# Expert stage of a four-layer network on one core: scatter before the hidden products, GpSimd multiplying the weights in, queries and scores two chunks ahead

## The chip, the cores and the metric

The kernel runs on one core of a Trainium2 chip. Its time is the device time of one execution in microseconds; the median of three runs counts. The names of the engines in the rows: PE is TensorE (PEld its weight loads), DVE is VectorE, ACT is ScalarE, POOL is GpSimd, SP the engine that issues the DMAs here.

## What is computed

The network is a chain of a bottleneck convolution, a spatial attention, a causal attention with the product-key expert layer below, another attention and a mixture of experts, on 16 images of 14 x 14 positions, 3136 tokens of 256 channels. The change touches only the product-key expert layer:

```python
def _L2_ffn_ref(x, norm_w, wq, keys, expert_down, expert_up):
    inv = jax.lax.rsqrt(jnp.mean(x * x, axis=-1, keepdims=True) + EPS)
    x_norm = x * inv * norm_w
    q = (x_norm @ wq).reshape(B, T, HEADS, 2, DIM_KEY)            # 8 heads, 2 x 32
    sim = jnp.einsum('bthpd,hkpd->pbthk', q, keys)                # 64 keys a half
    s1, i1 = jax.lax.top_k(sim[0], K)                             # K = 16
    s2, i2 = jax.lax.top_k(sim[1], K)
    all_idx = (i1[..., :, None] * NUM_KEYS + i2[..., None, :]).reshape(B, T, HEADS, K * K)
    all_scores = (s1[..., :, None] + s2[..., None, :]).reshape(B, T, HEADS, K * K)
    final_scores, pk = jax.lax.top_k(all_scores, K)
    final_idx = jnp.take_along_axis(all_idx, pk, axis=-1)
    hidden = jnp.einsum('btd,bthkd->bthk', x_norm, expert_down[final_idx])
    hidden = jax.nn.gelu(hidden, approximate=False)
    hidden = hidden * jax.nn.relu(final_scores)
    return jnp.einsum('bthk,bthkd->btd', hidden, expert_up[final_idx])
```

The kernel gathers nothing: it computes the hidden value of all 4096 experts for each token, and multiplies it with a matrix of weights that is zero but for the 128 chosen ones.

## The kernel before

`peer_ffn` holds the stage. 3136 tokens are 12 chunks of 256 tokens (two tiles of 128) and one of 64. Each engine has its own hand-written order of work, a function `chunk` that `chunks` calls: two chunks written out, a loop over pairs, then the last ones. Semaphores tie the engines together. Within an engine everything runs in the order in which it is written.

What one chunk n needs, and who does it:

- **Queries and scores** (`queries`, L1608, and `scores`, L1617, on TensorE; copies L1737 and L1744 on ScalarE): done for chunk n + 1 between the scatters of chunk n.
- **Search** (`top_halves`, VectorE, L1847 to L1854): for each tile the 16 best of 64 keys in 16 groups, by rounds of max, index and replace. Then GpSimd adds the candidates (`candidates`, L1552), VectorE searches them and makes the codes (`make_codes`, up to L1961) with the index steps of GpSimd (`index_steps`, L1557 to L1563).
- **Turn** (`turn`, L1639): TensorE transposes the codes of a tile, three transposes; ScalarE copies them out (L1780) into the bf16 rows `a_t`, `b_t` and `wh_t`; VectorE makes the low part `wl_t` of the weights (`low_weights`, L1966). There is one PSUM bank `tr_ps`, so the second tile's turn waits for the copies of the first and for its low weights.
- **Hidden** (`hidden`, L1630, 16 pairs of 4 matmuls; `hidden_out`, L1768): one pair after another into the four banks `x_ps`, Gelu from PSUM to `g`.
- **One-hots and scatter** (`one_hots`, L1988 to L1995, on VectorE; `scatter`, L1654 and L1655, on TensorE): 64 tokens (a `hb`) at a time, four of them in a chunk, each in four quarters, one `x_ps` bank a quarter. The weights of the experts of 16 tokens then lie in a bank.
- **Weights into g**: for the first two `hb` VectorE multiplies bank by bank (`weigh`, L2002, four behind the parts of the next one-hots). For the last two ScalarE copies the bank to `m_copy` (which is `qt`, L1790) and GpSimd multiplies it in (L1579).
- **Experts out** (`experts_out`, L1665, 64 matmuls into `out_ps`) and the addition to x (L2029) on VectorE.

TensorE's order in a chunk is: 10 pairs of hidden, the turns of both tiles, 6 pairs of hidden, scatter 0 with the queries behind it, scatters 1 and 2 with the scores behind them, scatter 3, experts out. VectorE's: low weights of tile 0, one-hots 0, low weights of tile 1, one-hots 1 to 3, both searches of the next chunk, its codes, the addition. A profile shows each matmul of hidden and experts out as two records, so each has 128 a chunk.

Of the kernel before, what the change touches and what calls it, by code (L numbers as in the profile page):

```python
# [7 lines left out]
ALU = mybir.AluOpType  # L8
# [6 lines left out]
P = 128  # L15
# [3 lines left out]
KC = C // P  # L19
# [1340 lines left out]
def peer_ffn(nc, x, xn_dram, mean_w, w, ident):  # L1360
# [15 lines left out]
    J = 32  # L1376
    HT = TT // 2
    NHB = 2 * NTILE
    LATE = NHB // 2
# [9 lines left out]
    with Scope(nc, "peer") as S:  # L1389
# [11 lines left out]
        m_copy = [qt[:, 2 * p:2 * p + 2, :].rearrange("p m t -> p (m t)") for p in range(2)]  # L1401
# [35 lines left out]
        g_done_late, m_copied = S.sem("g_done_late"), S.sem("m_copied")  # L1437
        halves_done, cand_ready = S.sem("halves_done"), S.sem("cand_ready")
# [3 lines left out]
        pad = S.sb("pad", [1, 1 + 3 * NTILE])  # L1442
# [19 lines left out]
        EARLY = 10  # L1462
# [7 lines left out]
        def chunks(eng, chunk):  # L1470

            for p in range(2):
                chunk(p, p, CT, CT)
            with eng.Fori(1, NCHUNK // 2 - 1) as i:
                for p in range(2):
                    chunk(2 * i + p, p, CT, CT)
            for p in range(2):
                chunk(NCHUNK - 2 + p, p, CT, CT if p == 0 else REST)
            chunk(NCHUNK, 0, REST, 0)
# [46 lines left out]
        def _(pool):  # L1526
# [38 lines left out]
            def next_tables(n, tiles):  # L1565

                for t in range(len(tiles)):
                    candidates(n, t)
                index_steps(n)

            next_tables(0, tile_rows(CT))

            def chunk(n, p, now, then):

                for hb in range(LATE, now // HT):
                    for q in range(4):
                        pool.wait_ge(m_copied, 4 * (NHB - LATE) * n + 4 * (hb - LATE) + q + 1)
                        ts = slice(hb * HT + q * GT, hb * HT + (q + 1) * GT)
                        nc.gpsimd.tensor_tensor(g[:, :, ts], g[:, :, ts], m_copy[q % 2].rearrange("p (t j) -> p j t", j=J),  # L1579
                                                ALU.mult).then_inc(g_done_late, 1)  # L1580
                if then > 0:
                    next_tables(n + 1, tile_rows(then))
# [3 lines left out]
        def _(pe):  # L1586
# [34 lines left out]
            def hidden(n, p, pairs, cols):  # L1621
                for jp in pairs:
                    b = jp % 4
                    if jp < 4:
                        wait(pe, m_copied, 4 * (NHB - LATE) * n - 3 + jp)
                    else:
                        pe.wait_ge(gelu_done, NPAIR * n + jp - 3)
# [14 lines left out]
            def scatter(n, hb):  # L1642

                pe.wait_ge(oh_ready, NHB * n + hb + 1)
                for q in range(4):
                    if hb == 0:
                        pe.wait_ge(gelu_done, NPAIR * (n + 1))
                    elif hb < LATE + 1:
                        pe.wait_ge(g_done, 4 * LATE * n + 4 * (hb - 1) + q + 1)
                    else:  # L1650
                        pe.wait_ge(m_copied, 4 * (NHB - LATE) * n + 4 * (hb - 1 - LATE) + q + 1)
# [6 lines left out]
            def experts_out(n, cols):  # L1658
                n_hb = cols // HT
                pe.wait_ge(g_done, 4 * LATE * n + 4 * min(LATE, n_hb))  # L1660
                pe.wait_ge(g_done_late, 4 * (NHB - LATE) * n + 4 * max(0, n_hb - LATE))
# [41 lines left out]
            def chunk(n, p, now, then):  # L1703
                hidden(n, p, range(EARLY), now)
                for t, rows in enumerate(tile_rows(now)):
                    turn(n, t, rows)
                hidden(n, p, range(EARLY, NPAIR), now)
                next_rows = tile_rows(then)
                for hb in range(now // HT):
                    scatter(n, hb)  # L1710
                    if hb == 0 and then > 0:
                        queries(n + 1, 1 - p, then)
                    if 0 < hb <= len(next_rows):
                        scores(n + 1, hb - 1, next_rows[hb - 1])
                experts_out(n, now)
# [3 lines left out]
        def _(act):  # L1719
# [21 lines left out]
            def score_out(n, t, rows):  # L1741
                act.wait_ge(sim_done, NTILE * n + t + 1)
                for b in range(2):
# [21 lines left out]
            def hidden_out(n, pairs, cols):  # L1765
                for jp in pairs:
                    act.wait_ge(h_done, NPAIR * n + jp + 1)
                    nc.scalar.activation(g[:, 2 * jp:2 * jp + 2, 0:cols], x_ps[jp % 4][:, 0:2 * CT].rearrange("p (j t) -> p j t", j=2)[:, :, 0:cols],  # L1768
                                         ACT.Gelu).then_inc(gelu_done, 1)

            def chunk(n, p, now, then):
                wait(act, out_done, n)
                hidden_out(n, range(EARLY), now)
                for t, rows in enumerate(tile_rows(now)):
                    act.wait_ge(tr_done, NTILE * n + t + 1)
                    ts = slice(t * TT, t * TT + rows)
                    if t == 0:
                        wait(act, oh_ready, NHB * n)
                    for dst, c in ((wh_t, 2), (a_t, 0), (b_t, 1)):
# [701 lines left out]
```

## Time and profile before

| | |
|---|---|
| three runs | 2382.08, 2389.36, 2386.52 us; median 2386.52 |
| span of the profiled execution | 2389.1 us |
| expert stage, about | 550 to 1862 us |
| busy: TensorE, VectorE, ScalarE, GpSimd | 79%, 70%, 28%, 19% of the span |
| granted TensorE clock, mean | 0.877 |

A row of a timeline gives the start in us, the time in us that a run of like instructions covers, engine, line, operation, output and inputs by name, shape, and in brackets how long the engine had been idle and on whom it waited. Instructions of an engine overlap by some 0.1 us, so the distance of two starts is what an instruction costs. In a row of windows the clock is the third number from the end: 1.00 is 2.4 GHz, 0.50 is 1.2 GHz.

### The profile page before, as it was taken

To read this page: it belongs to the slowest core of one execution; us is meant where nothing else is said; L and a number is where in the kernel's file an instruction comes from. 1 tells how busy PE (TensorE), PEld (TensorE's weight loads), DVE (VectorE), ACT (ScalarE), POOL (GpSimd) and SP (SyncE) were. 2 spreads that over 40 slices of the span, in tenths; PEclk is the share of its full clock that TensorE was granted. 3 is DMA by queue.
4 is the path that set the end of the run, shared out by engine and by line. 5 is a ranking of instruction groups with operands and counts; after the bars stand their busy time and mean duration, and the time that the engine had idled before them with its cause. 6 is when DMAs were issued, how large, how long until landed. Compare 5 with 4: busy or idle time off the path is not lost. (4 is left out here: it accounts for less than half of the span.)

```text
span 2389.1 us, 47903 instructions
## 1 busy us (share of the span) xinstructions
PE 1889.5 (79%) x17539; PEld 1539.2 (64%) x17539; DVE 1684.3 (70%) x6987; ACT 669.6 (28%) x1493; POOL 462.3 (19%) x667
## 2 busy tenths in 40 slices
PE   6595899996479788797787977978769699747995
PEld 3364688874468677686676866767658577544653
DVE  3433666645899999999999999999996477430112
ACT  1342355544222131121311213112120255421220
POOL 2002344330020201202112021120220311021111
PEclk8796899998789899898998988989888799858997
DMA  2232444413400000000000000000000233212434
GB/s 60 70 97 59 113 104 106 99 34 113 102 6 5 2 6 1 6 6 1 6 2 6 5 2 6 1 6 2 1 2 1 60 86 83 68 68 82 141 103 122
DMA packets 90420, 110.24 MB, mean 46 GB/s; under 512 B 27168, under 2 KB 79088, under 8 KB 89552
## 3 DMA queue, kind: packets, MB, share of 16 engines
q1 hardware_dynamic: 84672, 99.09, 15.8%
q0 software_dynamic: 3344, 6.53, 0.8%
q8 instruction: 140, 2.29, 0.4%
q10 hardware_dynamic: 2176, 1.61, 0.2%
q14 instruction: 88, 0.72, 0.1%
HBM read 69.84 MB, written 33.83 MB: 43 GB/s over the span
## 5 line engine op out<-in xcount | busy, mean ns | idle before, releaser
L1665 PE MATMUL peer_out_ps<-peer_g,peer_up 128*128 128x256 f32 (+1 forms) x1664 | 379.0, 393 | 85.1 <-issue 77.1
L1665 PEld LDWEIGHTS peer_out_ps<-peer_g,peer_up 128*128 128x128 f32 x1664 | 326.7, 203 | 133.8 <-issue 85.2
L1630 PE MATMUL peer_x_ps<-peer_xc,peer_dt 128*128 128x256 f32 (+1 forms) x1664 | 352.7, 373 | 19.6 <-DMA peer_up<-in_L_ffn_expert_up_dram 19.5
L1630 PEld LDWEIGHTS peer_x_ps<-peer_xc,peer_dt 128*128 128x128 f32 x1664 | 306.8, 191 | 60.3 <-issue 20.6
L1579 POOL TENSOR_TENSOR peer_g<-peer_g,peer_qt 128x512 f32<-128x512 f32 x96 | 153.0, 1636 | 796.0 <-ACT peer_qt L1790 796.0
L1768 ACT ACTIVATE peer_g<-peer_x_ps 128x512 f32<-128x512 f32 (+1 forms) x208 | 119.1, 573 | 637.1 <-PE peer_x_ps L1630 637.0
L1284 DVE TENSOR_REDUCE l_attn_mx<-l_attn_s_ps 98x4 f32<-98x392 f32 (+1 forms) x320 | 175.0, 560 | 142.7 <-PE l_attn_s_ps L1054 101.6
L1654 PE MATMUL peer_x_ps<-peer_oh_h,peer_oh_a 128*128 128x32 bf16 x3136 | 171.5, 181 | 111.2 <-DVE peer_oh_l L1995 95.6
L1654 PEld LDWEIGHTS peer_x_ps<-peer_oh_h,peer_oh_a 128*128 128x128 bf16 x3136 | 165.1, 99 | 128.5 <-DVE peer_oh_l L1995 63.5
L1988 DVE TENSOR_TENSOR peer_oh_a<-peer_a_t,peer_iota_f 128x8192 bf16<-128x8192 bf16 x49 | 216.6, 4421 | 1.3
L1205 ACT ACTIVATE l_attn_pt<-l_attn_st_ps 98x392 f32<-98x392 f32 x320 | 148.2, 492 | 147.1 <-PE l_attn_st_ps L1067 146.0
L1655 PE MATMUL peer_x_ps<-peer_oh_l,peer_oh_a 128*128 128x32 bf16 x3136 | 170.5, 181 | 0.0
L1852 DVE FIND_INDEX8 peer_i<-peer_v,peer_sc 128x8 uint32<-128x64 f32 (+1 forms) x800 | 166.3, 219 | 0.0
L1655 PEld LDWEIGHTS peer_x_ps<-peer_oh_l,peer_oh_a 128*128 128x128 bf16 x3136 | 165.2, 99 | 0.8
L1050 PE MATMUL l_attn_s_ps<-l_attn_stk,l_attn_stq 96*98 96x196 bf16 (+1 forms) x768 | 112.8, 244 | 31.7 <-DMA l_attn_stk<-l_attn_pieces_k_dram 18.6
L979 POOL TENSOR_SCALAR_AFFINE_SELECT l_attn_pt<-l_attn_pt 98x196 f32<-98x196 f32 (+1 forms) x192 | 98.5, 518 | 137.7 <-ACT l_attn_pt L1205 136.4
L1067 PE MATMUL l_attn_st_ps<-l_attn_stq,l_attn_stk 98*98 98x196 bf16 (+1 forms) x768 | 112.1, 244 | 8.9 <-ACT l_attn_pt L1205 4.5
L2428 DVE TENSOR_SCALAR moe_yt<-moe_b_ps,moe_b 128x392 f32<-128x392 f32 x16 | 10.0, 626 | 147.0 <-PE moe_b_ps L2251 147.0
L1847 DVE MAX8 peer_v<-peer_sc 128x8 f32<-128x64 f32 (+1 forms) x800 | 106.0, 210 | 1.3
L1088 PE MATMUL l_attn_o_ps<-l_attn_pt,l_attn_va 98*32 98x196 f32 (+1 forms) x1536 | 93.7, 315 | 9.3 <-DVE l_attn_o L1291 8.8
L1050 PEld LDWEIGHTS l_attn_s_ps<-l_attn_stk,l_attn_stq 96*98 96x98 bf16 x768 | 71.9, 128 | 44.2 <-DVE l_attn_mx L1284 23.1
L1067 PEld LDWEIGHTS l_attn_st_ps<-l_attn_stq,l_attn_stk 98*98 98x98 bf16 x768 | 71.4, 126 | 39.6 <-ACT l_attn_pt L1205 13.1
(325 smaller groups left out, 3460.4 us busy)
## 6 DMA issues: line engine op xcount, KB each, us to landing
moe_w<-in_L_ffn_w_dram SPq DMA_DIRECT2D x16, 1024.0 KB, 7.8
l_attn_pieces_q_dram<-l_attn_pieces_q SPq DMA_DIRECT2D x16, 294.0 KB, 3.9
l_attn_pieces_k_dram<-l_attn_pieces_k SPq DMA_DIRECT2D x16, 294.0 KB, 3.2
l_attn_stq<-l_attn_pieces_q_dram SPq DMA_DIRECT2D x16, 294.0 KB
l_attn_stk<-l_attn_pieces_k_dram SPq DMA_DIRECT2D x16, 294.0 KB
peer_g<-n_L_ffn_expert_down_dram SPq DMA_DIRECT2D x8, 512.0 KB
peer_up<-in_L_ffn_expert_up_dram SPq DMA_DIRECT2D x2, 2048.0 KB, 17.6
moe_expert_in<-l_blank SPq DMA_DIRECT2D x16, 197.5 KB
```

The lines of the kernel that those rows point to most:

```text
L1050: mm = nc.tensor.matmul(out[:, j, :], stq[n % NB][0:KS, spot(h), t * TH:(t + 1) * TH], stk[n % NB][0:KS, spot(h), 0:nb * TH], start=(j == ...
L1067: mm = nc.tensor.matmul(out[:, j, :], stk[n % NB][:, spot(h), u * TH:(u + 1) * TH], stq[n % NB][:, spot(h), t0 * TH:HW], start=(j == 0), s ...
L1205: nc.scalar.activation(pt[g % NPT][:, f * FW:(f + 1) * FW], st_ps[i % 2][0:TH, 0:FW], ACT.Exp).then_inc(exp_done, 1)
L1284: nc.vector.tensor_reduce(mx[n % 2][:, hs[0]:hs[0] + len(hs), t], s_ps[i % 2][0:TH, 0:FW].rearrange("p (h j) -> p h j", j=nb * TH), AX_X, ...
L1579: nc.gpsimd.tensor_tensor(g[:, :, ts], g[:, :, ts], m_copy[q % 2].rearrange("p (t j) -> p j t", j=J), ALU.mult).then_inc(g_done_late, 1)
L1630: mm = nc.tensor.matmul(x_ps[b][:, jj * CT:jj * CT + cols], dt[:, k, 2 * jp + jj, :], xc[p][:, k, 0:cols], start=(k == 0), stop=(k == KC - 1))
L1654: nc.tensor.matmul(x_ps[q][:, i * J:(i + 1) * J], oh_a[hb % 2][:, t, :], oh_h[hb % 2][:, t, :], start=True, stop=False)
L1655: mm = nc.tensor.matmul(x_ps[q][:, i * J:(i + 1) * J], oh_a[hb % 2][:, t, :], oh_l[hb % 2][:, t, :], start=False, stop=True)
L1665: mm = nc.tensor.matmul(out_ps[:, m * CT:m * CT + cols], up[:, j, m * P:(m + 1) * P], g[:, j, 0:cols], start=(j == 0), stop=(j == J - 1))
L1768: nc.scalar.activation(g[:, 2 * jp:2 * jp + 2, 0:cols], x_ps[jp % 4][:, 0:2 * CT].rearrange("p (j t) -> p j t", j=2)[:, :, 0:cols], ACT.Ge ...
L1852: last = nc.vector.max_index(indices[:, q, r], values[:, q, r], source)
L1988: nc.vector.tensor_tensor(view(oh_a[q]), spread(a_t, P), number(P), ALU.is_equal)
```

## The change

The scatter comes first in a chunk. ScalarE copies each scattered quarter straight into `g`. Hidden follows, Gelu goes to `act_out` (the memory of `qt`, two halves), and GpSimd multiplies pair by pair `act_out` into `g`. VectorE's `weigh` is gone. Experts out starts on a pair of rows as soon as its product is done (for m = 0), and has four places among its matmuls: queries of chunk n + 2 behind (m, j) = (0, 7), scores of its first tile behind (0, 20), the turns of chunk n + 1 behind (1, 3), scores of the second tile behind (1, 15). VectorE searches the first four groups of the next chunk before the low weights, and adds `out_ps` of the chunk before behind the first one-hots. GpSimd adds the candidates behind its products 5 and 11. One fold of the codes adds neighbours instead of halves, and a new semaphore `cand_read` keeps the scores from `sc` until the candidates in it have been searched. Queries, first scores and turns of the first chunks stand ahead of the loop.

```diff
@@ gpsimd
+            def weigh(n, jp, cols):
+                pool.wait_ge(gelu_done, NPAIR * n + jp + 1)
+                pair = g[:, 2 * jp:2 * jp + 2, 0:cols]
+                nc.gpsimd.tensor_tensor(pair, pair, act_out[jp % 2][:, :, 0:cols], ALU.mult).then_inc(g_done, 1)
+            def chunk(n, p, now, then, after):
+                tables = dict(zip((5, 11), range(len(tile_rows(then)))))
+                pool.wait_ge(m_copied, 4 * NHB * n + 4 * (now // HT))
+                for jp in range(NPAIR):
+                    weigh(n, jp, now)
+                    if jp in tables:
+                        candidates(n + 1, tables[jp])
                 if then > 0:
-                    next_tables(n + 1, tile_rows(then))
+                    index_steps(n + 1)
@@ tensor
-            def experts_out(n, cols):
...
+            def experts_out(n, p, cols, next_rows, after):
                 wait(pe, x_done, n)
+                after_rows = tile_rows(after)
                 for m in range(KC):
                     for j in range(J):
+                        if m == 0 and j % 2 == 0:
+                            pe.wait_ge(g_done, NPAIR * n + j // 2 + 1)
                         mm = nc.tensor.matmul(out_ps[:, m * CT:m * CT + cols], up[:, j, m * P:(m + 1) * P], g[:, j, 0:cols],
                                               start=(j == 0), stop=(j == J - 1))
-                mm.then_inc(out_done, 1)
+                        if m == KC - 1 and j == J - 1:
+                            mm.then_inc(out_done, 1)
+                        if (m, j) == QUERIES_AT and after > 0:
+                            queries(n + 2, p, after)
+                        if (m, j) == SCORES_AT and after > 0:
+                            scores(n + 2, 0, after_rows[0])
+                        if (m, j) == TURN_AT:
+                            for t, rows in enumerate(next_rows):
+                                turn(n + 1, t, rows)
+                        if (m, j) == LAST_SCORES_AT and len(after_rows) > 1:
+                            scores(n + 2, 1, after_rows[1])
...
+            queries(1, 1, CT)
+            scores(1, 0, TT)
+            for t in range(NTILE):
+                turn(0, t, TT)
+            scores(1, 1, TT)
+            def chunk(n, p, now, then, after):
                 for hb in range(now // HT):
                     scatter(n, hb)
...
+                hidden(n, p, now)
+                experts_out(n, p, now, tile_rows(then), after)
@@ scalar
+            def scattered(n, hb):
+                for q in range(4):
+                    act.wait_ge(m_done, 4 * NHB * n + 4 * hb + q + 1)
+                    ts = slice(hb * HT + q * GT, hb * HT + (q + 1) * GT)
+                    nc.scalar.activation(g[:, :, ts], x_ps[q][:, 0:GT * J].rearrange("p (t j) -> p j t", j=J), ACT.Copy).then_inc(m_copied, 1)
+            def hidden_out(n, cols):
+                for jp in range(NPAIR):
                     act.wait_ge(h_done, NPAIR * n + jp + 1)
+                    wait(act, g_done, NPAIR * n + jp - 1)
+                    nc.scalar.activation(act_out[jp % 2][:, :, 0:cols], ...
                                          ACT.Gelu).then_inc(gelu_done, 1)
+            def chunk(n, p, now, then, after):
                 wait(act, out_done, n)
+                for hb in range(now // HT):
+                    scattered(n, hb)
+                hidden_out(n, now)
+                after_rows = tile_rows(after)
+                if after > 0:
+                    act.wait_ge(g_done, NPAIR * (n + 1))
+                    query_out(n + 2, after)
+                    score_out(n + 2, 0, after_rows[0])
                 for t, rows in enumerate(tile_rows(then)):
+                    turned(n + 1, t, rows)
+                if len(after_rows) > 1:
+                    score_out(n + 2, 1, after_rows[1])
@@ vector
+                elif n == H // 4:
+                    pairs = m[:, 0:2 * n, :].rearrange("t (a b) k -> t b a k", b=2)
+                    chain.step(nc.vector.tensor_tensor(m[:, 0:n, :], pairs[:, 0, :, :], pairs[:, 1, :, :], ALU.add))
...
-                weigh_last(0)
                 chain.step(nc.vector.tensor_tensor(view(oh_l[q]), spread(b_t, J), number(J), ALU.is_equal))
-                weigh_last(1)
                 chain.wait()
                 nc.vector.tensor_tensor(view(oh_h[q]), view(oh_l[q]), spread(wh_t, J), ALU.mult)
-                weigh_last(2)
                 nc.vector.tensor_tensor(view(oh_l[q]), view(oh_l[q]), spread(wl_t, J), ALU.mult).then_inc(oh_ready, 1)
-                weigh_last(3)
...
+            def chunk(n, p, now, then, after):
...
+                if then > 0:
+                    top_halves(n + 1, 0, next_rows[0], last=EARLY)
                 low_weights(n, 0, tiles[0])
                 one_hots(n, 0)
                 if len(tiles) > 1:
                     low_weights(n, 1, tiles[1])
+                if not (isinstance(n, int) and n == 0):
+                    add_out(n - 1, CT)
+                for hb in range(1, n_hb):
+                    one_hots(n, hb)
                 if then > 0:
+                    for t, rows in enumerate(next_rows):
+                        top_halves(n + 1, t, rows, first=EARLY if t == 0 else 0)
+                    make_codes(n + 1, next_rows)
```

## Rows read from the trace of the kernel before

**Rows 1.** The list of waits, 850 to 1800 us: total us, times, longest.
```profile
DVE peer_wl_t L1966 <- ACT peer_b_t L1780: 33.3, 10, 3.5
```

**Rows 2.** Timeline of VectorE: chunk 1, then the start of chunk 11.
```profile
754.13 0.69 DVE L1966 TENSOR_TENSOR peer_wl_t<-peer_tr_ps,peer_wh_t 128x512 bf16<-128x512 f32 x1 [3.61 <-ACT peer_b_t L1780]
...
763.41 4.41 DVE L1988 TENSOR_TENSOR peer_oh_a<-peer_a_t,peer_iota_f 128x8192 bf16<-128x8192 bf16 x1
...
773.54 4.42 DVE L1988 TENSOR_TENSOR peer_oh_a<-peer_a_t,peer_iota_f 128x8192 bf16<-128x8192 bf16 x1
...
783.67 4.42 DVE L1988 TENSOR_TENSOR peer_oh_a<-peer_a_t,peer_iota_f 128x8192 bf16<-128x8192 bf16 x1
...
791.54 0.22 DVE L1847 MAX8 peer_v<-peer_sc 128x8 f32<-128x64 f32 x1
...
819.50 1.12 DVE L1847 MAX8 peer_oh_a<-peer_sc 128x8 f32<-128x64 f32 x8
...
833.84 0.29 DVE L1922 TENSOR_SCALAR peer_oh_a<-peer_oh_a 128x256 f32<-128x256 f32 x1
...
848.51 0.59 DVE L1961 SCALAR_TENSOR_TENSOR peer_oh_a<-peer_oh_a 128x256 f32<-128x256 f32 x1
...
1744.11 0.69 DVE L1966 TENSOR_TENSOR peer_wl_t<-peer_tr_ps,peer_wh_t 128x512 bf16<-128x512 f32 x1 [3.47 <-ACT peer_b_t L1780]
```

**Rows 3.** Timeline of TensorE: hidden, both turns, queries, experts out.
```profile
740.83 11.17 PE L1630 MATMUL peer_x_ps<-peer_xc,peer_dt 128*128 128x256 f32 x51
751.83 0.49 PE L1639 MATMUL peer_tr_ps<-net_ident,peer_oh_a 128*128 128x128 f32 x3
754.97 0.52 PE L1639 MATMUL peer_tr_ps<-net_ident,peer_oh_a 128*128 128x128 f32 x3 [2.65 <-DVE peer_wl_t L1966]
...
769.83 3.70 PE L1608 MATMUL peer_sim_ps<-peer_xc,peer_wq 128*128 128x256 f32 x16
...
803.34 30.42 PE L1665 MATMUL peer_out_ps<-peer_g,peer_up 128*128 128x256 f32 x128 [7.16 <-issue]
```

**Rows 4.** Timeline of ScalarE: last copy of the first turned tile.
```profile
753.48 0.62 ACT L1780 ACTIVATE peer_b_t<-peer_tr_ps 128x512 bf16<-128x512 f32 x1
```

**Rows 5.** Timeline of GpSimd: products, candidates, last of the index steps.
```profile
791.00 12.25 POOL L1579 TENSOR_TENSOR peer_g<-peer_g,peer_qt 128x512 f32<-128x512 f32 x8 [66.81 <-ACT peer_qt L1790]
...
819.52 1.52 POOL L1552 TENSOR_TENSOR peer_sc<-peer_v 128x128 f32<-128x128 f32 x4 [12.40 <-DVE peer_pad L1903]
...
823.08 0.20 POOL L1563 CAST peer_oh_a<-peer_oh_a 128x16 bf16<-128x16 f32 x1
```

**Rows 6.** Windows: stretch, length, busy time of each engine, clock, DMA share, GB/s.
```profile
752.00:757.00 5.00, 2.35 (x14) 1.97 (x13) 2.76 (x2) 3.54 (x7) 0.00 (x0) 1.00 0.00 0
...
783.00:784.00 1.00, 0.79 (x29) 0.79 (x30) 1.00 (x3) 0.00 (x0) 0.00 (x0) 0.50 0.00 0
...
788.00:789.00 1.00, 1.00 (x6) 0.76 (x4) 1.00 (x2) 0.00 (x0) 0.00 (x0) 0.98 0.00 0
...
803.00:804.00 1.00, 0.66 (x2) 0.60 (x3) 1.00 (x12) 0.00 (x0) 0.24 (x1) 0.50 0.00 0
...
808.00:809.00 1.00, 1.00 (x5) 0.80 (x5) 1.00 (x12) 0.00 (x0) 0.00 (x0) 0.74 0.00 0
```

**Rows 7.** Timeline of VectorE: codes and first low weights of chunk 0.
```profile
647.39 0.60 DVE L1961 SCALAR_TENSOR_TENSOR peer_oh_a<-peer_oh_a 128x256 f32<-128x256 f32 x1
655.08 0.69 DVE L1966 TENSOR_TENSOR peer_wl_t<-peer_tr_ps,peer_wh_t 128x512 bf16<-128x512 f32 x1 [7.08 <-ACT peer_b_t L1780]
```

**Rows 8.** The last 64 tokens: hidden, a window of experts out, the addition.
```profile
1823.30 9.04 PE L1630 MATMUL peer_x_ps<-peer_xc,peer_dt 128*128 128x64 f32 x80
...
1850.00:1861.00 11.00, 11.00 (x100) 10.95 (x99) 0.00 (x0) 0.00 (x0) 0.00 (x0) 1.00 0.01 1
...
1861.13 0.29 DVE L2029 TENSOR_TENSOR net_x<-net_x,peer_out_ps 128x128 f32<-128x128 f32 x1 [14.60 <-PE peer_out_ps L1665]
```

**Rows 9.** GpSimd's products in chunk 11: ns shortest, median, longest.
```profile
L1579 POOL TENSOR_TENSOR peer_g<-peer_g,peer_qt x8: 1492/1522/5607, 1774.9 to 1791.3; 128x512 f32<-128x512 f32 x8
```

**Rows 10.** Timeline of VectorE beside them: the last one-hots' product.
```profile
1781.55 2.50 DVE L1995 TENSOR_TENSOR peer_oh_l<-peer_oh_l,peer_wl_t 128x2048 bf16<-128x2048 bf16 x1
```

More of the change, by code:

```diff
@@ L1378, in peer_ffn @@
     NHB = 2 * NTILE
-    LATE = NHB // 2
     GT = HT // 4
@@ L1472, in chunks @@
             for p in range(2):
-                chunk(p, p, CT, CT)
+                chunk(p, p, CT, CT, CT)
             with eng.Fori(1, NCHUNK // 2 - 1) as i:
                 for p in range(2):
[L1476 to L1479, printed above, removed]
+                    chunk(2 * i + p, p, CT, CT, CT)
+            chunk(NCHUNK - 2, 0, CT, CT, REST)
+            chunk(NCHUNK - 1, 1, CT, REST, 0)
+            chunk(NCHUNK, 0, REST, 0, 0)
         def tile_rows(tokens):
@@ L1563, in index_steps @@
                     nc.gpsimd.tensor_copy(step16[:, half, 0, :], entries[:, 0, :]).then_inc(steps_ready, 1)
[L1565 to L1580, printed above, removed]
+            def weigh(n, jp, cols):
[3 more added lines that the diff above has]
+            for t in range(NTILE):
+                candidates(0, t)
+            index_steps(0)
+            def chunk(n, p, now, then, after):
[5 more added lines that the diff above has]
+                        candidates(n + 1, tables[jp])
                 if then > 0:
-                    next_tables(n + 1, tile_rows(then))
+                    index_steps(n + 1)
             chunks(pool, chunk)
@@ L1619, in scores, with hidden @@
                 mm.then_inc(sim_done, 1)
-            def hidden(n, p, pairs, cols):
-                for jp in pairs:
+            def hidden(n, p, cols):
+                for jp in range(NPAIR):
                     b = jp % 4
                     if jp < 4:
-                        wait(pe, m_copied, 4 * (NHB - LATE) * n - 3 + jp)
+                        pe.wait_ge(m_copied, 4 * NHB * n + 4 * (cols // HT) - 3 + jp)
                     else:
@@ L1701, in _ @@
             pe.wait_ge(w_in, 16 * 4)
[L1703 to L1708, printed above, removed]
+            queries(1, 1, CT)
+            scores(1, 0, TT)
+            for t in range(NTILE):
+                turn(0, t, TT)
+            scores(1, 1, TT)
+            def chunk(n, p, now, then, after):
                 for hb in range(now // HT):
                     scatter(n, hb)
[L1711 to L1715, printed above, removed]
+                hidden(n, p, now)
+                experts_out(n, p, now, tile_rows(then), after)
             chunks(pe, chunk)
@@ L1742, in score_out @@
                 act.wait_ge(sim_done, NTILE * n + t + 1)
+                wait(act, cand_read, n)
                 for b in range(2):
@@ L1767, in hidden_out @@
+            def hidden_out(n, cols):
+                for jp in range(NPAIR):
                     act.wait_ge(h_done, NPAIR * n + jp + 1)
[L1768 removed]
+                    wait(act, g_done, NPAIR * n + jp - 1)
+                    nc.scalar.activation(act_out[jp % 2][:, :, 0:cols], x_ps[jp % 4][:, 0:2 * CT].rearrange("p (j t) -> p j t", j=2)[:, :, 0:cols],
                                          ACT.Gelu).then_inc(gelu_done, 1)
[L1771 to L1790 removed]
@@ new lines, in turned @@
+            def turned(n, t, rows):
+                act.wait_ge(tr_done, NTILE * n + t + 1)
+                ts = slice(t * TT, t * TT + rows)
+                if t == 0:
+                    wait(act, oh_ready, NHB * n)
+                for dst, c in ((wh_t, 2), (a_t, 0), (b_t, 1)):
+                    ins = nc.scalar.activation(dst[:, ts, :], tr_ps[:, c * TT:c * TT + rows].unsqueeze(2).broadcast_to([P, rows, R]), ACT.Copy)
+                ins.then_inc(tr_ready, 1)
+            query_out(1, CT)
@@ L1893, in fold, with top_halves @@
                     chain.step(nc.vector.tensor_tensor(out, m[:, 0, :], m[:, 1, :], ALU.add))
-            def top_halves(n, t, rows):
+            def top_halves(n, t, rows, first=0, last=G16):
                 dve.wait_ge(sim_ready, NTILE * n + t + 1)
                 nc.vector.memset(pad[:, 1 + t:2 + t], 0.0)
-                groups = slice(t * G16, (t + 1) * G16)
-                top16(v16[0:rows, groups, :], i16[0:rows, groups, :], [sc[t][0:rows, q, :] for q in range(G16)])
-                chain.wait()
-                nc.vector.memset(pad[:, 3 + t:4 + t], 0.0).then_inc(halves_done, 1)
+                groups = slice(t * G16 + first, t * G16 + last)
+                top16(v16[0:rows, groups, :], i16[0:rows, groups, :], [sc[t][0:rows, q, :] for q in range(first, last)])
+                if last == G16:
+                    chain.wait()
+                    nc.vector.memset(pad[:, 3 + t:4 + t], 0.0).then_inc(halves_done, 1)
             def make_codes(n, tiles):
@@ L1920, in make_codes @@
                 chain.wait()
+                nc.vector.memset(pad[:, 7:8], 0.0).then_inc(cand_read, 1)
                 wait(dve, tr_done, NTILE * n)
```

63 lines of the change are left out of this document (18 added, 45 removed).

## Prediction

> **What bounds the kernel now.** The page comes first: VectorE is busy in nine tenths or more of every slice of the expert stage, TensorE in seven or eight. The list of waits for the stage then says what is left of VectorE's idle time: one wait a chunk, 33.3 us in ten, for the columns that ScalarE copies after the codes are turned [rows 1]. The timeline of VectorE shows one chunk end to end [rows 2]: the low-weight copy that opens a chunk (L1966) starts at 754.13 and, ten chunks later, at 1744.11, so a period is 99.0 us. VectorE sets it: about 95.4 us of work and 3.6 us of that wait. The timeline of TensorE [rows 3] shows what the other big engine would need, and rows 4 to 6 what ScalarE, GpSimd and TensorE's clock do.
>
> **What VectorE loses and gains.** Write C for the end of the codes of the next chunk, L for the start of its first low-weight copy, X for the start of the addition of out_ps. One-hots with four weight products among them take 773.54 to 783.67, 10.13 us; without, 783.67 to 791.54, 7.87 us [rows 2]. Two such sets a chunk lose them: 4.5 us off. Those products go to ScalarE (a PSUM copy in its place) and GpSimd. The 3.6 us wait goes too, because four groups of the next search are done meanwhile. Sixteen groups twice take 791.54 to 819.50, 27.96 us, or 0.87 us a group; cutting 4 off costs one more set of waits, which I take as 0.3 us (bounds 0 and 0.6). The other ordering of one fold reads the same 1024 elements: 0, bounds plus or minus 0.1. The extra one-element memset costs under 0.1. Pure work is then 99.0 - 3.6 - 4.5 + 0.4 = 91.3 us.
>
> **The new wait.** The addition of out_ps moves from the end of a chunk to a place after the first one-hots of the next. It waits for the last matmul of the experts' output, and that one now sits behind the turning of the codes in TensorE's order (turn after m=1, j=3; 28 matmuls and the second scores behind it). The second tile's turn also still waits for VectorE's first low-weight copy, as it does now (2.65 us idle) [rows 3], and VectorE makes that copy only after the four early groups. So, from C:
> - early groups 4 x 0.87 + 0.3 = 3.8, less the 0.15 by which instructions overlap: L = C + 3.6. The copies that it needs are there earlier: turn starts at 751.83, the third copy ends at 754.10 [rows 4], 2.3 us, so C + 2.5.
> - the second turn starts 0.84 after L (754.13 to 754.97) and takes some 0.36; then 28 matmuls, each two records of 0.216 us (11.17 us for 51, with the pipeline's end) [rows 3], 12.1 us; the scores, 8 records, 1.8 us; and 0.2 to the addition: X = L + 15.3 at full clock.
> - VectorE itself is ready at L + 9.3 (754.13 to 763.41 is just copy, one-hots, copy [rows 2]). It therefore stands still for 6.0 us, with three sets of one-hots, both searches and the next codes queued behind.
>
> **The clock** adds to this. TensorE reaches the turn before the codes are there (next part), so it is nearly idle from C - 1.7 to C + 4.8, 6.5 us, with only three transposes in it. A gap of 2.65 us left it at 2.4 GHz (1.00 in the rows) [rows 6]. After 7.16 us idle it restarted at 1.2 GHz (0.50) and came back only about 5 us later, and its 128 records took 30.42 instead of 27.6, 2.8 us more [rows 3, 6]; the scatter that began at half clock in 783 to 784 saw full clock again at 788 [rows 6]. The bounds of the loss are thus 0 and 2.8 us; I take 2.1, nearer the long gap, because the fall comes during the gap and the recovery varies (from 4.5 us at half clock 2.2 are lost).
>
> **The period.** From X to C: addition 0.6, three one-hots 3 x 7.87 = 23.6, the remaining 12 groups 10.5, the second tile 14.0, the candidates' top 16 14.35 (819.50 to 833.84), codes 15.1 (833.84 to the end of L1961 at 849.1, less overlap) [rows 2], 0.1 for the memset: 78.2. Then 3.6 to L and 15.3 + 2.1 to X: **99.2 us**, against 99.0. The 8.1 us taken off come back as 6.0 of waiting and 2.1 of slow clock.
>
> **Does another engine come later?** TensorE, from X: the fourth one-hots are ready at 24.2; scatter 3.2 after 0.15 (its earlier quarters wait for nothing); hidden 128 records, 27.6, and 0.4 for a slow start; 36 matmuls 15.6; queries 3.6 [rows 3]; scores 1.8: 76.5, so 1.7 before C. It has slack of 3.6 + 1.7 - 2.4 = 2.9 us to L. GpSimd: a product of 512 elements takes 1.53 us (12.25 for 8), candidates 1.5, index steps 2.3 (819.52 to 823.28, less the candidates) [rows 5]. TensorE gives it a pair each 1.73 us (8 records), so the sixth product starts 2.65 + 5 x 1.73 = 11.3 us after hidden and ends at 12.8; two candidates steps and ten products back to back make it 31.1. That is X + 59.1, and X + 61.4 with the steps; VectorE begins the codes at X + 63.1 and reads the steps at X + 66. Free by 1.7 us. The wide chunk load, issued after hidden, has 3.5 us before the queries read it, about what it takes now beside the scatter; 0, bounds 0 and 1, inside TensorE's slack. ScalarE gets 16 copies and loses none of its others but 8: it is 28% busy, and its new wait for all products stands only ahead of query and score copies that have over 10 us. Queries and scores two chunks ahead thus cost nothing and gain nothing: no wait of VectorE for scores stands in the rows.
>
> **Head and tail.** Codes of chunk 0 end at 648.0, and VectorE waits 7.08 us until 655.08, since ten pairs of hidden are ahead of the turn [rows 7]. After, L is 648.0 + 3.6 = 651.6. Chunk 0 has no addition to wait for: 0.8 + 7.87 + 0.6 + 23.6 + 10.5 + 14.0 + 14.35 + 15.2 + 3.6 = 90.6, so the L of chunk 1 is 742.2, **11.9 earlier** than 754.13. Ten periods follow: **+2.0**. At the end hidden is no longer done ahead of the scatter. Before, from the L of chunk 11 to the last addition it is 1861.13 - 1744.11 = 117.0 [rows 2, 8]. After: addition at 15.4 (no second scores, clock 2.1), fourth one-hots 39.8, scatter 43.1, hidden 71.1, all 64 output matmuls with the turn among them 99.1, the last scatter 102.3 (its one-hots are long ready), hidden of the 64 tokens 16 x 0.89 = 14.3 (9.04 us for 10 pairs), output 128 records at 0.11 = 14.1 [rows 8], 0.3: 131.1, **+14.1**.
>
> Sum: -11.9 + 2.0 + 14.1 = +4.2 us on the profiled span of 2389.1. That execution is 2.6 us over the median of 2386.5, within the spread of the runs, so 4.2 goes on the median: **2390.7 us**. A difference under 0.3% (7 us) can't be told from none here.
>
> **Rivals.** *(a) The clock stays up*: the three transposes and the short work around the turn suffice. For it: the 2.65 us gap. Against: twice as long a gap here. Period 97.1, ten times -1.9, so 2390.7 - 21 = 2370. Chance 0.2. *(b) The wait isn't there*, if the out matmuls that it waits for are done sooner than the order says; then 8.1 us a chunk come off: 91 us, 2390.7 - 80 = 2310. Only if the program's order were not kept, or TensorE finished the rest in 9 us; chance 0.03. *(c) GpSimd slips into the codes.* In chunk 11 products met one-hots: one took 5.607 us [rows 9] and the one-hots' product beside it 2.50 instead of 1.22 [rows 10]. If a product takes over about 1.70 us in place of 1.53, or hidden begins 1.7 us later, the index steps start in VectorE's codes part. From there, each collision costs VectorE about 1.3 us, two or three of them a chunk, and steps_ready comes late: 3 us a chunk, 2390.7 + 30 = 2421. Against it: such products run beside searches in all other chunks and take 1.53. Chance 0.15. The Trainium skill, page "SBUF — State Buffer", section "Who interferes with whom", says that a VectorE instruction with two SBUF inputs and a GpSimd one that reads SBUF block each other for a whole instruction, while one with one SBUF input doesn't; the 5.607 us agree with that. By that rule the products beside the searches are safe and only the last 1.7 us of slack count.
>
> **How the numbers follow.** The forecast has 0.62; within it the clock's loss of 0 to 2.8 and the 0.3 to 0.6 of the others move a period by some 1 us, the sum by 10. Range 2366 to 2413, which holds (a) and part of (c). Faster by over 0.3%: (a), (b) and 0.07 of the forecast, 0.30. Slower: (c) and 0.15 of it, 0.30. Within: 0.40.
>
> **What would show it.** L2029's successor on VectorE waits for TensorE 6 to 9 us in each chunk; the wait for L1780's copies is gone; the first L1966 of a chunk comes 3.6 us after the codes; TensorE has 1 to 2 us of waiting for the codes, and half clock behind the turn; products on GpSimd stay at 1.53 us; hidden of chunk 0 begins some 55 us later. Wrong if additions don't wait, if TensorE comes to the turn after the codes, or if GpSimd is the releaser of anything on VectorE.

## The result, and the profile after

The changed kernel takes **2401.96 us** (median of five runs, 2393.71 to 2405.38) against 2386.52 before: 1.0065 of the time, with a 95% interval of 1.0047 to 1.0084. It is slower by 15.4 us. The prediction was 2390.7, range 2366 to 2413. The range holds the result; the likeliest case, "no difference that can be told", does not.

The head of the page of the changed kernel, and its slices of VectorE and of the clock:

```profile
span 2400.0 us, 48197 instructions
PE 1871.1 (78%) x17539; PEld 1533.4 (64%) x17539; DVE 1631.4 (68%) x6948; ACT 734.0 (31%) x1593; POOL 557.9 (23%) x779
DVE  3433576646998988989889898998985377430112
PEclk8687899998588979879798897988989799957997
```

VectorE has less to do (68% of the span for 70%), and yet the slices of the stage go up and down between 8 and 9. Where the idle time sits is told by the waits of VectorE between 850 and 1750 us (columns: engine, tile and line that waited, who released it; us in total, times, longest):

```profile
DVE net_x L2024 <- PE peer_out_ps L1664: 67.6, 9, 8.0
DVE peer_pad L1926 <- issue: 9.8, 3, 3.4
```

The one wait of before, for ScalarE's copies of the turned codes [rows 1], is gone. In its place stand two: the addition of out_ps (L2024) waits in every chunk, 7.3 to 8.0 us and 7.5 on the mean (forecast 8.1), and the first search (L1926, its one-element memset) stands still three times for about 3.3 us with nothing to wait for that the profile shows ("issue"), which nobody forecast. VectorE's timeline shows a chunk without that stop and one with it (start, duration, line, operation, tiles; in brackets the idle time ahead and its releaser):

```profile
938.13 0.59 DVE L1990 SCALAR_TENSOR_TENSOR peer_oh_a<-peer_oh_a 128x256 f32<-128x256 f32 x1
...
938.66 0.06 DVE L1926 MEMSET peer_pad<- 1x1 f32 x1
...
942.34 0.67 DVE L1995 TENSOR_TENSOR peer_wl_t<-peer_tr_ps,peer_wh_t 128x512 bf16<-128x512 f32 x1
...
950.99 0.68 DVE L1995 TENSOR_TENSOR peer_wl_t<-peer_tr_ps,peer_wh_t 128x512 bf16<-128x512 f32 x1
959.37 0.69 DVE L2024 TENSOR_TENSOR net_x<-net_x,peer_out_ps 128x512 f32 x1 [7.70 <-PE peer_out_ps L1664]
...
1037.41 0.58 DVE L1990 SCALAR_TENSOR_TENSOR peer_oh_a<-peer_oh_a 128x256 f32<-128x256 f32 x1
...
1041.24 0.06 DVE L1926 MEMSET peer_pad<- 1x1 f32 x1 [3.25 <-issue]
...
1045.04 0.67 DVE L1995 TENSOR_TENSOR peer_wl_t<-peer_tr_ps,peer_wh_t 128x512 bf16<-128x512 f32 x1
```

L1990 ends the codes (C), the first L1995 is L, L2024 is X. The end of the codes to L is 3.6 us in the first chunk (938.72 to 942.34) and 7.1 in the second (1037.99 to 1045.04). The second stretch is where the written loop over chunks 2 to 9 goes from one round to the next. Two chunks make a round, so in four rounds there are three such places: ahead of the L at 1045.04, 1246.76 and 1448.12. From one L to the next it is 99.1 us on the mean of the seven plain chunks (98.6 to 99.6) and 102.4 to 102.7 in those three (942.34 to 1045.04: 102.7).

TensorE around the same turn, in its timeline:

```profile
933.68 3.19 PE L1664 MATMUL peer_out_ps<-peer_g,peer_up 128*128 128x256 f32 x14
938.97 0.52 PE L1640 MATMUL peer_tr_ps<-net_ident,peer_oh_a 128*128 128x128 f32 x3 [2.10 <-DVE peer_oh_a L1990]
943.16 0.87 PE L1640 MATMUL peer_tr_ps<-net_ident,peer_oh_a 128*128 128x128 f32 x3 [3.67 <-DVE peer_wl_t L1995]
943.82 6.76 PE L1664 MATMUL peer_out_ps<-peer_g,peer_up 128*128 128x256 f32 x24
950.42 1.89 PE L1618 MATMUL peer_sim_ps<-peer_keys_b,peer_qt 128*128 128x256 f32 x8
952.14 7.07 PE L1664 MATMUL peer_out_ps<-peer_g,peer_up 128*128 128x256 f32 x32
```

and the windows over it (window, its length; busy time and count of PE, PEld, DVE, ACT, POOL; granted clock, DMA share, GB/s):

```profile
938.00:939.00 1.00, 0.03 (x1) 0.06 (x2) 1.00 (x7) 0.00 (x0) 0.00 (x0) 1.00 0.00 0
...
940.00:941.00 1.00, 0.00 (x0) 0.00 (x0) 0.96 (x11) 1.00 (x3) 0.00 (x0) 0.50 0.00 0
...
945.00:946.00 1.00, 1.00 (x4) 0.73 (x4) 1.00 (x1) 0.64 (x2) 0.00 (x0) 0.50 0.00 0
...
947.00:948.00 1.00, 1.00 (x6) 0.90 (x5) 1.00 (x2) 0.00 (x0) 0.00 (x0) 1.00 0.00 0
```

TensorE comes to the turn 2.1 us before the codes and waits 3.67 us more for L1995 before the second tile; in between its clock falls to 1.2 GHz (0.50), and in 945 to 946 it still makes 4 records a microsecond where 947 to 948 has 6. Both are the forecast picture.

Over the whole stage, from the L of chunk 1 to that of chunk 11:

```profile
743.15:1744.70 1001.55, 790.39 (x8060) 700.96 (x8060) 901.70 (x4541) 254.89 (x440) 252.13 (x290) 0.85 0.01 4
```

That is 901.70 us of VectorE's work in 1001.55, 90.2 of 100.2 a chunk. The rest, 10 us a chunk, is idle: 7.5 of it the wait for the addition, 1 the stops (3 x 3.3 us in ten chunks), what is left gaps too short for the list of waits.

| part | forecast | measured |
|---|---|---|
| L of chunk 1, before 754.13 | 742.2 (-11.9) | 743.15 (-11.0) |
| ten periods, before 990.0 | +2.0 | 1001.6 (+11.6) |
| L of chunk 11 to the last addition, before 117.0 | 131.1 (+14.1) | 132.9 (+15.9) |
| sum, to the last addition | +4.2 | +16.5 (1861.13 to 1877.65) |

The spans differ by 10.9 only, since what follows the stage took 522.3 us in this execution and 528.0 in that of before. The code there is the same in both. Another execution with the old expert stage (e2 below) took 524.3 from its last addition (1866.71) to its end (2391.0), so a few microseconds of that part come and go from one execution to the next. The sum of +16.5 in the stage stands against +15.4 between the medians.

### The profile page after: what moved, and what is told of

It reads as the page before. It is cut to its first block and busy times, and to the rows that moved or that the text cites. A ratio compares the mean times of both kernels' runs of the same rounds, so it can differ in the third digit from the quotient of the medians.

```text
span 2400.0 us, 48197 instructions
## 1 busy us (share of the span) xinstructions
PE 1871.1 (78%) x17539; PEld 1533.4 (64%) x17539; DVE 1631.4 (68%) x6948; ACT 734.0 (31%) x1593; POOL 557.9 (23%) x779
## 5 line engine op out<-in xcount | busy, mean ns | idle before, releaser
L1569 POOL TENSOR_TENSOR peer_g<-peer_g,peer_qt 128x512 f32<-128x512 f32 (+1 forms) x208 | 250.7, 1213 | 930.2 <-ACT peer_qt L1783 930.1
L1664 PE MATMUL peer_out_ps<-peer_g,peer_up 128*128 128x256 f32 (+1 forms) x1664 | 369.8, 382 | 0.0
L1664 PEld LDWEIGHTS peer_out_ps<-peer_g,peer_up 128*128 128x128 f32 x1664 | 316.4, 197 | 43.6 <-issue 0.4
L1777 ACT ACTIVATE peer_g<-peer_x_ps 128x512 f32<-128x512 f32 x196 | 117.3, 598 | 315.0 <-PE peer_x_ps L1654 314.4
L1783 ACT ACTIVATE peer_qt<-peer_x_ps 128x512 f32<-128x512 f32 (+1 forms) x208 | 119.2, 573 | 231.0 <-PE peer_x_ps L1631 230.4
L1088 PE MATMUL l_attn_o_ps<-l_attn_pt,l_attn_va 98*32 98x196 f32 (+1 forms) x1536 | 91.3, 307 | 9.5 <-DVE l_attn_o L1291 8.9
```

Of the source, the lines that this page charges most:

```text
L1569: nc.gpsimd.tensor_tensor(pair, pair, act_out[jp % 2][:, :, 0:cols], ALU.mult).then_inc(g_done, 1)
L1777: nc.scalar.activation(g[:, :, ts], x_ps[q][:, 0:GT * J].rearrange("p (t j) -> p j t", j=J), ACT.Copy).then_inc(m_copied, 1)
L1783: nc.scalar.activation(act_out[jp % 2][:, :, 0:cols], x_ps[jp % 4][:, 0:2 * CT].rearrange("p (j t) -> p j t", j=2)[:, :, 0:cols], ACT.Gelu ...
```

## The experiments

The theory after the first reading: nearly all of it is as forecast but for a term of 3 x 3.3 us, the jump back of the written loop, which before lay inside the 3.6 us wait. Each run's kernel has its own line numbers, shifted by its edit: the addition is L2024 in the changed kernel and L2023 with the loop written out. The rivals: the memset or the cut after four groups costs this by itself; or the stop is the same in both kernels and the loss is elsewhere (GpSimd, the clock).

**The loop written out in the changed kernel** (e1_unroll_after):

```diff
-            with eng.Fori(1, NCHUNK // 2 - 1) as i:
-                for p in range(2):
-                    chunk(2 * i + p, p, CT, CT, CT)
+            for n in range(2, NCHUNK - 2):
+                chunk(n, n % 2, CT, CT, CT)
```

> The changed kernel with its loop over chunks 2 to 9 written out on TensorE, ScalarE, VectorE and GpSimd. Theory: the 3.25 us that VectorE stands idle ahead of the first search of chunks 4, 6 and 8 is the jump back to the start of the loop, and nothing covers it since the wait for the turned codes is gone; then the three stalls go, about 10 us off, 2392 us, and ten periods of 99.2 us instead of three of 102.6 and seven of 99.1. Rival: it is a wait for the scores that ScalarE copies; then it stays, in the written-out chunks too, 2402 us.

Measured: 2393.37 us (2385.27 to 2399.38, ten runs), 1.0029 of before (1.0012 to 1.0045), 8.6 below the changed kernel, whose interval (1.0047 to 1.0084) doesn't meet this one. VectorE's timeline at the place that had the stop, and its only wait between 850 and 1700:

```profile
1030.66 0.58 DVE L1989 SCALAR_TENSOR_TENSOR peer_oh_a<-peer_oh_a 128x256 f32<-128x256 f32 x1
...
1031.18 0.06 DVE L1925 MEMSET peer_pad<- 1x1 f32 x1
...
1034.86 0.67 DVE L1994 TENSOR_TENSOR peer_wl_t<-peer_tr_ps,peer_wh_t 128x512 bf16<-128x512 f32 x1
...
DVE net_x L2023 <- PE peer_out_ps L1663: 68.7, 9, 7.7
```

The memset and the cut are still there and the stop is not; the ten periods are 99.0 to 99.2. The stop belongs to the loop. Which part of going round it takes the time, no run here tells.

**The loop written out in the kernel before** (e2_unroll_before): the same edit in the old code.

> The kernel before with the same loop written out. Theory: its jump back lies inside the 3.6 us wait for the turned codes, so nothing is gained: 2386 us, within 3 us. Rival: the jump costs there as well, and 10 us come off: 2376 us.

Measured: 2389.13 us (2380.89 to 2397.87, ten runs), 1.0008 (0.9990 to 1.0025): no difference. The wait that covered the jump stays in all nine chunks:

```profile
DVE peer_wl_t L1965 <- ACT peer_b_t L1779: 31.1, 9, 3.5
```

So the jump cost nothing that can be told in the old kernel, and in the new one taking it out gave 8.6 us. Together the two runs show the missing term from both sides.

**The addition one set of one-hots later** (e3_add_later). This moves the addition off the place where TensorE can't be done yet:

```diff
-                if not (isinstance(n, int) and n == 0):
-                    add_out(n - 1, CT)
                 for hb in range(1, n_hb):
                     one_hots(n, hb)
+                    if hb == 1 and not (isinstance(n, int) and n == 0):
+                        add_out(n - 1, CT)
+                if n_hb == 1:
+                    add_out(n - 1, CT)
```

> The changed kernel with the addition of out_ps behind the second one-hots instead of the first. Theory: VectorE's 7.4 us wait for TensorE is the place of the addition; moved, the second one-hots run in it, and the third then wait for the first scatter only until 20.5 us after the low weights, so 5.4 us a chunk come off: 2402 - 59 = 2343 us. Rival: TensorE's own chain (out, scatter, hidden, out) sets the period and the wait moves to the turn: under 10 us off, 2392 us or more.

Measured: 2347.09 us, 0.9827 (0.9804 to 0.9850), 4 above what was expected. VectorE's waits between 850 and 1700:

```profile
DVE peer_oh_a L2014 <- PE peer_x_ps L1654: 22.4, 9, 3.2
DVE peer_pad L1926 <- issue: 9.9, 3, 3.4
DVE net_x L2024 <- PE peer_out_ps L1664: 4.0, 6, 0.9
```

The wait for the output falls from 7.5 us a chunk to under 1. The three stops are still there. Of the gain 2.5 us a chunk go back at once: the third set of one-hots needs the buffer of the first, and the scatter that reads it sits behind the same output matmuls on TensorE. Periods without a stop are 93.3 to 95.7, and ten of them, stops and all, take 955.7 us for 1001.6.

**The turn of the codes later on TensorE** (e4_turn_later), so that fewer output matmuls are behind it:

```diff
-        QUERIES_AT, SCORES_AT, TURN_AT, LAST_SCORES_AT = (0, 7), (0, 20), (1, 3), (1, 15)
+        QUERIES_AT, SCORES_AT, TURN_AT, LAST_SCORES_AT = (0, 7), (0, 20), (1, 11), (1, 15)
```

> The changed kernel with the turns behind matmul (1, 11) instead of (1, 3). Theory: 8 matmuls fewer lie between the turn and the addition (3.5 us), TensorE reaches the turn 1.8 us after the codes instead of 1.9 before, its gap shrinks to the 2.6 us between the two turns and the clock stays up: period 94.3, about 50 us off, 2350 us. Rival: TensorE is the bound, and a later turn moves the start of the low weights by the 3.5 us: no gain, 2402 us.

Measured: 2366.07 us, 0.9914 (0.9889 to 0.9940); better than the changed kernel by 36 us, and 16 short of what was expected. The wait fell to 4.1 us a chunk and not to about 2.6. The reason is in TensorE's timeline and the windows:

```profile
931.34 0.49 PE L1640 MATMUL peer_tr_ps<-net_ident,peer_oh_a 128*128 128x128 f32 x3
934.39 0.79 PE L1640 MATMUL peer_tr_ps<-net_ident,peer_oh_a 128*128 128x128 f32 x3 [2.56 <-DVE peer_wl_t L1995]
...
933.00:934.00 1.00, 0.00 (x0) 0.00 (x0) 1.00 (x6) 0.52 (x2) 0.00 (x0) 1.00 0.00 0
...
936.00:937.00 1.00, 1.00 (x4) 0.82 (x3) 1.00 (x1) 0.80 (x2) 0.00 (x0) 0.50 0.00 0
...
938.00:939.00 1.00, 1.00 (x6) 0.90 (x5) 1.00 (x2) 0.00 (x0) 0.00 (x0) 1.00 0.00 0
```

In a plain chunk TensorE no longer waits for the codes, only 2.56 us (2.5 to 2.8 in all of them) for L1995, no longer than the 2.65 after which the kernel before kept 2.4 GHz [rows 6]. Here the clock fell all the same, and the matmuls behind the gap began at half speed. It did so in each of the ten periods. A gap that left the clock up in one kernel takes it down in another.

**TensorE kept busy at the turn** (e5_busy_turn): matmuls that nobody reads, four ahead of the first turn and seven between the turns. They are added work.

```diff
+            def keep_busy(count):
+                for _ in range(count):
+                    nc.tensor.matmul(x_ps[3][:, 0:CT], up[:, 0, 0:P], wq[:, 0, 0:CT], start=True, stop=True)
...
+                            pe.wait_ge(gelu_done, NPAIR * (n + 1))
                             for t, rows in enumerate(next_rows):
+                                keep_busy(4 if t == 0 else 7)
                                 turn(n + 1, t, rows)
```

> The changed kernel with matmuls that nobody reads (128x256 f32, into a free bank): 4 ahead of the first turn of a chunk and 7 between its turns, where TensorE idles. Theory: the gap around the turn drops the clock to half, and the matmuls behind it lose 1.7 to 2.1 us a chunk; kept busy, the clock stays up, VectorE's wait for the addition falls from 7.4 to 5.5 us, about 19 us off, 2383 us. Rival: the slow clock costs nothing or the extra matmuls delay the turn: 2402 us or more.

Measured: 2393.42 us (2384.80 to 2398.81, ten runs), 1.0025 (1.0009 to 1.0042), 8.5 below the changed kernel and 10 above what was expected. In a plain chunk it does what was forecast. The second turn and the output matmuls behind it, and a window over these:

```profile
931.76 0.52 PE L1640 MATMUL peer_tr_ps<-net_ident,peer_oh_a 128*128 128x128 f32 x3 [0.64 <-DVE peer_wl_t L2001]
932.12 5.34 PE L1668 MATMUL peer_out_ps<-peer_g,peer_up 128*128 128x256 f32 x24
...
936.00:937.00 1.00, 1.00 (x6) 0.89 (x5) 1.00 (x2) 0.00 (x0) 0.00 (x0) 1.00 0.00 0
```

The clock stays at 1.00 (also from 927 to 932, over the turns themselves), the 24 records take 5.34 us in place of 6.76, the addition waits 5.97 us (forecast for full clock: 6.0), and the period is 97.6. The clock is thus worth 99.1 - 97.6 = 1.5 us a chunk. At the three places of the jump TensorE has 3.3 us more to wait (4.1 in place of 0.6 to 0.8), the clock falls there too, and the additions wait 7.4 to 8.8. That is where the rest of the expected gain stayed.

**Eight early groups in place of four** (e6_early8: `EARLY = 8`).

> The changed kernel with eight groups of the next search ahead of the low weights instead of four. Theory: four more groups put off the low weights by 3.5 us, and with them the second turn and the last matmul, and take 3.5 us from behind the addition: nothing is gained, 2402 us, within 5. Rival: they fill VectorE's wait, 3.5 us a chunk off: 2365 us.

Measured: 2403.45 us, 1.0062 of before, the same as the changed kernel. L comes 7.0 us after the codes in place of 3.6, and the addition waits as long as ever: TensorE's matmuls start that much later too, and the groups done early are missing later. The early search moves work and wins none.

**GpSimd's slack** (e9_pool_later, e10_pool_much_later): 6 and 18 small products that nobody reads, ahead of GpSimd's index steps.

```diff
...
                 if then > 0:
+                    for i in range(18):
+                        wait(pool, spared, 18 * n + i)
+                        nc.gpsimd.tensor_tensor(spare[:, :], wq[:, 0, 0:128], wq[:, 1, 0:128], ALU.mult).then_inc(spared, 1)
                     index_steps(n + 1)
```

> The changed kernel with six small products that nobody reads (128x128 f32, about 0.5 us each) on GpSimd ahead of its index steps, 3 us a chunk. In the changed kernel the steps end 6.5 us before VectorE reads them, and 3.4 before it begins the codes. Theory: GpSimd has this slack, 2402 us, within 4. Rival: GpSimd is already on the path, 3 us a chunk: 2435 us.

> The same with eighteen, 9 us a chunk, which is past the slack: the steps then meet the codes on VectorE and come 2.5 us after they are wanted. Theory: 3 to 5 us a chunk, 2435 to 2455 us, with a wait of VectorE for GpSimd in each chunk. Rival: TensorE's and VectorE's wait for the addition takes it up: 2402 us.

The cut shows the run with 18; in the other it says 6. Measured: 2405.08 us for 6 of them, 1.0078 (1.0061 to 1.0095), 3 above the changed kernel; and 2488.99 us for 18, 1.0419, above all that was expected (2435 to 2455). The longer one in GpSimd's and VectorE's timelines, and in VectorE's waits between 850 and 1700:

```profile
1040.66 11.33 POOL L1586 TENSOR_TENSOR peer_spare<-peer_wq 128x128 f32<-128x128 f32 x18
...
1049.40 0.67 DVE L1964 TENSOR_TENSOR peer_oh_a<-peer_oh_a 128x256 f32<-128x256 f32 x1
...
1054.28 1.83 DVE L1909 TENSOR_TENSOR peer_oh_a<-peer_oh_a 128x2048 bf16<-128x2048 bf16 x2 [4.21 <-POOL peer_oh_a L1564]
...
DVE net_x L2028 <- PE peer_out_ps L1668: 68.8, 8, 8.9
DVE peer_oh_a L1909 <- POOL peer_oh_a L1564: 32.6, 8, 4.2
```

So the mechanism of rival (c) exists, but the ten periods of the changed kernel are far from it: with 6 products the plain periods are still 98.6 to 99.5, with 18 most are some 106. Its price was put too low. Besides the 4.2 us wait for the index steps, the addition waits 1.4 us longer, 8.8 for 7.4.

**Both moves, with the loop and without** (e7_both: the edit of e3_add_later and TURN_AT at (1, 8); e8_both_unroll: the same with the loop written out).

> The changed kernel with the addition behind the second one-hots and the turns behind matmul (1, 8). Theory: no wait is left on VectorE but the jump back: a period of 91.2 us, 8 us a chunk off, 2402 - 88 = 2314 us. Rival: TensorE becomes the bound at about 94 us: 2402 - 55 = 2347 us.

> The same with the loop written out. Theory: another 10 us, 2304 us. Rival: written-out code costs as much as the jump: 2314 us.

Measured: 2325.04 us, 0.9732 (0.9704 to 0.9760), and 2310.62 us (2307.06 to 2321.89), **0.9689 (0.9656 to 0.9723)**, 11 and 7 above what was expected. The second is 3.1% faster than the kernel before and the fastest of all. Its slices of VectorE, and its only wait between 850 and 1700:

```profile
DVE  3433566653999999999999999999982677320112
...
DVE peer_oh_a L2013 <- PE peer_x_ps L1653: 4.0, 3, 1.4
```

Seven of its ten periods are 91.3 to 91.5 us, which is the pure work of the forecast (91.3); the three with that wait are 92.6 to 92.8. The jump costs more in e7 than 3.3 us a time: its periods with a jump are 94.9 to 95.2, and the ones behind them 93.1 to 93.9, since the third one-hots wait 1.4 to 2.3 us there. The difference of the two medians is 14.4 us.

## Why the prediction was right, and where it failed

**The step that failed is the one that costed the removed wait.** The prediction says "The 3.6 us wait goes too" and takes all of it off in every chunk, then asks only whether TensorE, ScalarE or GpSimd come later. It did not ask what VectorE itself was doing in the wait. In three of ten periods it was going around the written loop, 3.2 to 3.4 us without an instruction, which a wait of 3.6 us hid. With the wait gone that is paid: 3 x 3.3 = 9.9 us, of the 12.3 by which the stage exceeds the forecast. Shown by e1 (8.6 us off the median) and e2 (nothing). The trace of before could have led there: the expert stage has a loop in the code, and none of its waits was put down to it.

That the range held is in part luck: its width was given to the clock and to small terms, none of it to this one, and the jump alone took 9.9 of the 22 us up to its edge.

Of the remaining 2.4 us, after 0.3 that the periods gave back (the plain ones were 99.1 for 99.2):

- *Head*, 0.9 too hopeful: the last step of the codes of chunk 0 starts at 648.35, not 647.39 [rows 7], and L follows after 3.6 us (652.55), as forecast. From this L to the next it is 90.6, as forecast. The same step starts at 642.65 in e1, whose work up to there is the same, so the place of the whole head moves by some microseconds from one run to another.
- *Tail*, 1.8 too hopeful. The route of the forecast (scatter, hidden, output one after the other) holds, but chunk 11's codes for the last 64 tokens come later than it assumed. The prediction gave the tail no line for GpSimd, and named GpSimd as a releaser of VectorE as a sign that it was wrong: here it is one. VectorE's waits between 1760 and 1880, without the two for the additions:

```profile
DVE peer_pad L1940 <- POOL peer_sc L1552: 8.3, 1, 8.3
DVE peer_oh_a L1905 <- POOL peer_oh_a L1563: 3.5, 1, 3.5
DVE peer_wl_t L1995 <- ACT peer_b_t L1792: 1.5, 1, 1.5
```

  The candidates for those tokens stand behind products on GpSimd, and VectorE, whose search is done, has nothing to put in between: 8.3 and 3.5 us. Most of it falls in time that the tail waits for TensorE anyway (the last addition waits 31.13 us for L1664). TensorE itself waits 1.06 us for these codes, at their turn (1833.12), and ends hidden of chunk 11 71.8 us after L for the 71.1 of the forecast. That these two are the 1.8 us was not tried.

**What held:**

- *Pure work 91.3 us.* VectorE is busy 90.2 a chunk, and e8, which has hardly a wait, has a period of 91.5.
- *L = C + 3.6.* Exactly so in every plain chunk (938.72 to 942.34).
- *The new wait.* X = L + 17.4 was forecast; it is 17.5 in the first of the ten chunks and falls to 16.6 in the last of them. The addition waits 7.3 to 8.0 us for a forecast of 8.1. The move bought 8.1 us a chunk and a wait gave them back, which was the main claim. e3 shows it by taking the wait away.
- *The split into 6.0 of order and 2.1 of clock.* With the clock held up (e5) the wait is 5.97. The clock's part was a little large: 1.5 to 1.7 measured.
- *TensorE reaches the turn 1.7 us before the codes*: 2.1 at 938.97, 1.5 to 2.4 between 830 and 1650.
- *Period 99.2*: 99.1 on the mean of the seven plain chunks.

**The rivals.** (a) *The clock stays up*, 2370: false, it falls to 0.50 in every turn. Its price was sized rightly (97.1; e5's plain period is 97.6), and its argument from the 2.65 us gap was weaker than it looked, as e4 shows. (b) *No wait*: false. e3 and e7 show what the changed kernel is with less or none of it: 2347 and 2325. The forecast of 2310 had no term for the jump either; without the loop it is 2311 (e8). (c) *GpSimd slips into the codes*: not in the ten periods. GpSimd's products of 512 elements, by form, between 850 and 1750 (number, shortest/median/longest in ns, first and last start):

```profile
L1569 POOL TENSOR_TENSOR peer_g<-peer_g,peer_qt x144: 1260/1267/1284, 891.0 to 1719.2; 128x512 f32<-128x512 f32 x144
```

They take 1.27 us each and not the 1.53 that rows 5 gave. The layouts differ: the old product read its second operand across rows, 32 elements apart, the new one reads two runs of 256 tokens from both (that this makes the difference was not tried alone). The error was harmless; it made the slack larger (index steps done 3 us before the codes begin, not 1.7). None of the 144 met a blocked stretch: the spread is 24 ns, and VectorE was in its searches beside every one of them.

In the tail it did happen. The last products of chunk 11 ran beside VectorE's codes for the last 64 tokens:

```profile
1810.68 1.25 DVE L1955 TENSOR_SCALAR peer_oh_a<-peer_oh_a 128x256 f32<-128x256 bf16 x1
...
1812.26 3.96 DVE L1896 TENSOR_TENSOR peer_oh_a<-peer_oh_a,peer_starts_b 128x2048 bf16<-128x2048 bf16 x2
...
1813.78 4.98 POOL L1569 TENSOR_TENSOR peer_g<-peer_g,peer_qt 128x512 f32<-128x512 f32 x3 [0.31 <-ACT peer_qt L1783]
```

In a plain chunk L1955 takes 0.29 us and the two of L1896 1.82. So rival (c) was false for the periods and true for this one set of codes, where most of its cost lay under TensorE's work.

The Trainium skill, page "SBUF — State Buffer", section "Who interferes with whom", says that a VectorE instruction with two inputs in SBUF and a GpSimd one that reads SBUF hold each other up, while one with a single input does not, outside the modes in which VectorE uses both of its ports. The 144 products beside the searches agree with the second half. The first half agrees with L1896 in the tail, and with e10, where a VectorE step with two inputs took 0.67 us instead of 0.42 beside GpSimd's products. L1955 has a single input and took 1.25 us beside a product all the same, so counting inputs alone would have misled here; whether it ran in such a mode, the trace does not say.

**The chances.** The result, 0.65% slower, lies 0.35% beyond the edge of "no difference". The prediction gave slower 0.3, all of it by GpSimd and by slips of single terms; a term for something hidden under the removed wait was missing, and with it the slower side would have had more than the faster one.

## What to carry to other kernels

When a wait is removed, list what its own engine did under it and not only who comes late next: here a loop's jump cost nothing inside a wait and its full price outside. And when work is taken off the engine that sets the pace, look at which of its instructions now comes before its producer can be done; moving that one (here the addition, by one set of one-hots, with the turn moved to match) turned a loss of 0.6% into a gain of 2.7%, and of 3.1% with the loop written out.

## What the runs showed of the hardware that was not expected

- Going round a written loop costs VectorE 3.1 to 3.4 us without an instruction here, seen as "issue" ahead of the first memset of the next round (nine of nine times in after, e3 and e4). With about 3.5 us of waiting at the same place it costs nothing (e2).
- TensorE's clock fell after a gap of 2.56 us in one kernel (e4) and stayed up after 2.65 in another [rows 6]. The length of the last gap alone did not decide it.
- VectorE's steps of the codes beside GpSimd's products in the tail: 1.25 us for 0.29 (one input), 3.96 for 1.82 (two steps of two inputs). The 144 products beside searches took 1.26 to 1.28 us, all of them.
- A GpSimd product of 512 f32 elements took 1.27 us with runs of 256 tokens and 1.53 with an operand read 32 elements apart [rows 5].
